# Square roots of the norms moved from ScalarE to four-step Newton iterations on VectorE in a two-layer gated cross-attention kernel

## What is computed

```python
def _layernorm(x, axis=-1, eps=1e-05):
    m = jnp.mean(x, axis=axis, keepdims=True)
    v = jnp.var(x, axis=axis, keepdims=True)
    return (x - m) / jnp.sqrt(v + eps)

x = x + jnp.tanh(g_xattn[0]) * _L0_xattn_ref(_layernorm(x), ctx_1024, ...)
x = x + jnp.tanh(g_ffn[0]) * _L0_ffn_ref(_layernorm(x), ...)
x = x + jnp.tanh(g_xattn[1]) * _L1_xattn_ref(_layernorm(x), ctx_1024, mask, ...)
x = x + jnp.tanh(g_ffn[1]) * _L1_ffn_ref(_layernorm(x), ...)
```

```python
def _ln(t, w, b):
    m = jnp.mean(t, axis=-1, keepdims=True)
    v = jnp.var(t, axis=-1, keepdims=True)
    return (t - m) * jax.lax.rsqrt(v + EPS) * w + b
```

## Time and profile before

| | us |
|---|---|
| time, median of 3 runs | 1687.81 (1685.54 to 1689.53) |
| the profiled execution | 1685.9 |
| its span, first to last instruction | 1684.5 |
| busy in the span: PE, DVE, ACT, POOL | 1454.9, 1229.2, 1127.1, 792.1 |
| mean granted clock of PE | 0.942 of full speed |

### The profile page before, as it was taken

One profiled execution on the slowest core, in us unless ns is written; L12 is line 12 of the kernel. 1 busy time (PEld: TensorE's weight loads), 2 busy tenths in 40 slices (PEclk: granted clock), 3 DMA queues, 4 the chain that ended last, 5 costly groups with the idle time before them and its releaser, 6 DMA issues.

```text
span 1684.5 us, 25330 instructions
## 1 busy us (share of the span) xinstructions
PE 1454.9 (86%) x8374; PEld 711.7 (42%) x8460; DVE 1229.2 (73%) x2184; ACT 1127.1 (67%) x2020; POOL 792.1 (47%) x615
## 2 busy tenths in 40 slices
PE   5687988888888887688898989899899999999979
PEld 3243343343333343244444444344544455455445
DVE  6765766666686356478887768899589997788937
ACT  3567667667764755477787668678477775788724
POOL 3014013014030001078766749787486877577823
PEclk8798997897999999799999999999999999999989
DMA  4001200200340100100000100000000000000000
GB/s 154 1 1 39 43 1 11 50 1 1 60 176 1 51 1 5 39 21 6 1 1 23 38 20 6 26 1 1 6 26 1 26 1 1 1 1 1 1 1 26
DMA packets 20488, 36.69 MB, mean 22 GB/s; under 512 B 4898, under 2 KB 15238, under 8 KB 19334
## 3 DMA queue, kind: packets, MB, share of 16 engines
q1 hardware_dynamic: 20358, 35.07, 7.2%
HBM read 26.53 MB, written 1.15 MB: 16 GB/s over the span
## 4 chain that ended last, share of the span: by engine, by line
PE 35%; POOL 9%; issue 7%; DVE 5%; ACT 3%; POOLq 0%; DMA 0%; ACTq 0%; DVEq 0%; SPq 0%
PE BK L582 35%; POOL arena L1878 6%; DVE arena L1514 3%; DVE arena L1497 1%; ACT arena L1760 1%; ACT arena L1768 1%; POOL arena L1875 1%; POOL arena L1853 1%; ACT arena L1753 1%; POOL arena L1884 1%; POOL arena L1863 1%; DVE arena L886 0%; PE BK L866 0%; ACT L1753 0%; DVE arena L1528 0%
## 5 line engine op out<-in xcount | busy, mean ns | idle before, releaser
L582 PE MATMUL BK<-arena 128*128 128x512 bf16 (+10 forms) x8044 | 1407.2, 378 | 192.6 <-DVE arena L1497 30.6
L582 PEld LDWEIGHTS BK<-arena 128*128 128x128 bf16 (+7 forms) x8130 | 674.2, 115 | 894.8 <-issue 235.1
L1878 POOL TENSOR_TENSOR arena<-arena 128x512 f32<-128x512 f32 (+1 forms) x352 | 509.5, 1447 | 178.6 <-ACT arena L1753 154.5
L1514 DVE TENSOR_TENSOR arena<-arena 128x512 bf16<-128x512 f32 (+1 forms) x416 | 514.4, 1245 | 39.7 <-ACT arena L1760 38.8
L1753 ACT ACTIVATE arena<-BK,arena 128x512 f32<-128x512 f32 (+1 forms) x416 | 285.9, 687 | 132.3 <-PE BK L582 117.1
L1329 DVE TENSOR_REDUCE arena<-BK 128x1 f32<-128x512 f32 x384 | 244.0, 683 | 65.6 <-PE BK L582 64.4
L1661 ACT ACTIVATE arena<-BK 128x512 f32<-128x512 f32 (+1 forms) x416 | 226.0, 598 | 76.0 <-PE BK L582 69.6
L1760 ACT CAST arena<-arena 128x512 bf16<-128x512 f32 (+1 forms) x416 | 253.3, 609 | 0.0
L1768 ACT ACTIVATE arena<-BK 128x512 bf16<-128x512 f32 (+1 forms) x256 | 130.0, 508 | 87.8 <-PE BK L582 86.7
L1497 DVE CUSTOM_DVE_ANT_0 arena<-BK,arena 128x512 bf16<-128x512 f32 (+1 forms) x256 | 145.7, 569 | 47.4 <-PE BK L582 37.5
L1802 POOL TENSOR_TENSOR arena<-arena 128x256 f32<-128x256 f32 (+6 forms) x45 | 30.2, 671 | 208.1 <-ACT arena L1600 205.7
(11 more groups left out here) (170 smaller groups left out, 863.8 us busy)
## 6 DMA issues: line engine op xcount, KB each, us to landing
arena<-arena SPq DMA_DIRECT2D x144, 50.0 KB, 2.2
arena<-in_ctxT SPq DMA_DIRECT2D x8, 800.5 KB, 4.4
arena<-in_ctxk SPq DMA_DIRECT2D x4, 768.0 KB
arena<-in_wo SPq DMA_DIRECT2D x1, 2048.0 KB, 7.9
arena<-in_wqT SPq DMA_DIRECT2D x1, 2048.0 KB, 7.7
arena<-in_x SPq DMA_DIRECT2D x4, 256.0 KB, 11.0
arena<-in_rsel SPq DMA_DIRECT2D x1, 1024.0 KB, 9.2
arena<-in_rw1T SPq DMA_DIRECT2D x1, 1024.0 KB, 5.1
```

The lines of the kernel that those rows point to most:

```text
L582: return T.matmul(out_, lhsT, rhs, start=start, stop=stop, skip_group_check=True)
L1514: V.tensor_tensor(Pl[k][0:m, :], P1[k][0:m, :], Ph[k][0:m, :], ALU.subtract).then_inc(p_low, 1)
L1878: G.tensor_tensor(acc[0:m, g % 2, :], acc[0:m, g % 2, :], P1[k][0:m, :], ALU.add).then_inc(summed1, 1)
```

## The change

- All roots of the head norms but batch 0's are taken on DVE as inverse roots: a first estimate from the bits of the number, and three Newton steps, in four pieces `nw`. The reciprocals of `scale` fall away with them, and POOL's multiplication waits for the root alone.
- Eight of the 16 roots of the x norms (`STEPPED`: turn 1 batches 0 to 2, turn 2 batches 2 and 3, turn 3 batches 0 to 2) are taken the same way in four pieces `nr`.
- The statistics and ACT roots of turn 0 for batches 1 to 3 stand ahead of batch 0's `sqrt`, and x is loaded ahead of the context of batch 1.
- In stage 2 the norms leave `bg` and `og` and have a queue `late` of their own, drawn from in four of every 13 steps. `rest(8)` keeps the places that they had in `bg` empty.

```diff
+STEPPED = ((1, 0), (1, 1), (1, 2), (2, 2), (2, 3), (3, 0), (3, 1), (3, 2))
...
-        to.append(("ln1", turn, b))
-        yield
+        if turn or b == 0:
+            to.append(("ln1", turn, b))
+            yield
+        if (turn, b) in STEPPED:
+            for part in range(4):
+                to.append(("nr", turn, b, part))
+                yield
...
-            for _ in range(2 if b else 1):
-                yield
-            piece("sqrt", b)
             if b:
                 yield
+                yield
+                for part in range(4):
+                    piece("nw", b, part)
+                    yield
+            else:
+                for later in range(1, B):
+                    piece("ln1", 0, later)
+                yield
+                piece("sqrt", b)
...
-        bg = chain(context(1), values(1), masked(1), self.norm(to, 2, 2), self.norm(to, 2, 3), context(2), values(2),
+        bg = chain(context(1), values(1), masked(1), rest(8), context(2), values(2),
...
-        og, paced = iter(()), [0]
+        og, late, paced = iter(()), chain(self.norm(to, 2, 2), self.norm(to, 2, 3)), [0]
...
-                og = chain(finish(g - 1), self.norm(to, 3, (g - 1) // 8) if g % 8 == 0 else None)
+                og = finish(g - 1)
+                if g % 8 == 0:
+                    late = chain(late, self.norm(to, 3, (g - 1) // 8))
...
+            if kt % 13 in (11, 12, 0, 1):
+                next(late, None)
...
+        def dve_root_step(x, y, t, part, done):
+            dve.wait_ge(dve_chain.sem, dve_chain.n)
+            if part == 0:
+                V.tensor_scalar(y.bitcast(I32), x.bitcast(I32), -0.5, 1597463007.0, ALU.mult,
+                                ALU.add).then_inc(dve_chain.sem, dve_chain.up())
+            else:
+                V.tensor_tensor(t, y, y, ALU.mult).then_inc(dve_chain.sem, dve_chain.up())
+                dve.wait_ge(dve_chain.sem, dve_chain.n)
+                V.scalar_tensor_tensor(out=t, in0=t, scalar=-0.5, in1=x, op0=ALU.mult,
+                                       op1=ALU.mult).then_inc(dve_chain.sem, dve_chain.up())
+                dve.wait_ge(dve_chain.sem, dve_chain.n)
+                u = V.scalar_tensor_tensor(out=y, in0=t, scalar=1.5, in1=y, op0=ALU.add, op1=ALU.mult)
+                u.then_inc(*((done, 1) if part == 3 else (dve_chain.sem, dve_chain.up())))
+
+        def dve_norm_root(turn, b, part):
+            sl = slice(2 * b, 2 * b + 2)
+            if part == 0:
+                dve.wait_ge(stat1, 8 * (turn - 1) + 2 * b + 2)
+                V.tensor_scalar(rsq[:, sl], mv[:, sl, 1], 1e-5, None, ALU.add).then_inc(dve_chain.sem, dve_chain.up())
+            dve_root_step(rsq[:, sl], rst[:, sl], rtt[:, :], part, root1)
...
+                elif kind == "nw":
+                    b, part = arg
+                    x, t = (sq[:, k, :].rearrange("p (k h) -> p k h", h=H) for k in range(2))
+                    if part == 0:
+                        for j in range(5):
+                            dve.wait_ge(*summed(5 * b + j))
+                        V.tensor_scalar(x, ss[:, :, :], 1.0 / 16, 1e-6, ALU.mult,
+                                        ALU.add).then_inc(dve_chain.sem, dve_chain.up())
+                    dve_root_step(x, ss[:, :, :], t, part, ss_root)
...
-            SP.dma_start(ctxT[:, 1, :], a["ctxT"][1]).then_inc(ld_ctx[1], 16)
             for b in range(1, B):
                 SP.dma_start(x_sb[:, 2 * b:2 * b + 2, :], xv[:, 2 * b:2 * b + 2, :]).then_inc(ld_x[b], 16)
+            SP.dma_start(ctxT[:, 1, :], a["ctxT"][1]).then_inc(ld_ctx[1], 16)
```

More of the change, by code:

```diff
@@ L8 @@
 U8 = mybir.dt.uint8
+I32 = mybir.dt.int32
 ALU = mybir.AluOpType
@@ L429, in finish, with rest @@
                     yield
+        def rest(n):
+            for _ in range(n):
+                yield
         for _ in values(0):
             pass
-        bg = chain(context(1), values(1), masked(1), self.norm(to, 2, 2), self.norm(to, 2, 3), context(2), values(2),
+        bg = chain(context(1), values(1), masked(1), rest(8), context(2), values(2),
                    context(3), values(3), masked(2), ternary(0), masked(3), ternary(1, 2))
-        og, paced = iter(()), [0]
+        og, late, paced = iter(()), chain(self.norm(to, 2, 2), self.norm(to, 2, 3)), [0]
         mgs = chain(*[gen(g + n) for g in range(NG) for gen, n in ((self.maxima, 1), (self.qproj, 2)) if g + n < NG])
@@ L467, in stage2 @@
             pace(2)
-        for _ in chain(og, finish(NG - 1), bg):
+        for _ in chain(og, late, finish(NG - 1), bg):
             pass
@@ L595, in program @@
         rsq = sb("rsq", [128, NT])
+        rtt = sb("rtt", [128, 2])
         xn = sb("xn", [128, 2, D])
@@ L835, in dve_norm_apply @@
             dve.wait_ge(root1, 4 * (turn - 1) + b + 1) if turn else dve.wait_ge(root0, b + 1)
-            V.reciprocal(rst[:, sl], rsq[:, sl]).then_inc(dve_chain.sem, dve_chain.up())
-            dve.wait_ge(dve_chain.sem, dve_chain.n)
+            if (turn, b) not in STEPPED:
+                V.reciprocal(rst[:, sl], rsq[:, sl]).then_inc(dve_chain.sem, dve_chain.up())
+                dve.wait_ge(dve_chain.sem, dve_chain.n)
             if turn and norm_before(turn, b):
@@ L1253, in vector_main @@
                     dve_norm_stats(*arg)
+                elif kind == "nr":
+                    dve_norm_root(*arg)
                 elif kind == "ln2":
                     dve_norm_apply(*arg)
+                elif kind == "nw":
[7 more added lines that the diff above has]
+                    dve_root_step(x, ss[:, :, :], t, part, ss_root)
                 elif kind == "kv":
@@ L1285, in vector_main @@
                     lo, hi, m = ((14, 16, 128), (0, 4, 128), (4, 8, 128), (8, 12, 128), (12, 14, TAIL))[r]
-                    dve.wait_ge(ss_root, b + 1)
-                    V.reciprocal(ss[:, lo:hi, :], ss[:, lo:hi, :]).then_inc(ss_recip, 1)
                     if b == 0:
+                        dve.wait_ge(ss_root, 1)
+                        V.reciprocal(ss[:, lo:hi, :], ss[:, lo:hi, :]).then_inc(ss_recip, 1)
                         v = kc[0:m, lo:hi, :].rearrange("p k (h d) -> p (k h) d", d=16)
@@ L1577, in scalar_main @@
                 i, n = slot.get(piece, (None, None))
-                if kind == "ln1":
+                if kind == "ln1" and arg not in STEPPED:
                     act_norm_root(*arg)
@@ L1599, in scalar_main @@
                     act.wait_ge(*summed(u - 2)) if u >= 2 else act.wait_ge(rsb_done, 1)
+                    act.wait_ge(ss_root, b)
                     A.activation(sq[0:m, 4 * k:4 * k + hi - lo, :], kc[0:m, lo:hi, :], ACT.Square).then_inc(squared, 1)
@@ L1811, in gpsimd_main @@
                     v = kc[0:m, lo:hi, :].rearrange("p k (h d) -> p (k h) d", d=16)
-                    pool.wait_ge(ss_recip, 5 * b + r + 1)
+                    pool.wait_ge(ss_root, b + 1)
                     G.tensor_tensor(v, v, ss[0:m, lo:hi, :].rearrange("p k h -> p (k h)").unsqueeze(2)
```

## The result

The median of four runs is 1716.26 us (1708.12 to 1717.68), beside 1688.67 for the kernel before: a ratio of 1.016, 95% interval 1.0139 to 1.0181. The change costs 27.6 us, where a gain of 10.3 was forecast, and the time lies outside the range. The profiled execution (1708.1, span 1706.7) is the fastest of the four. Its mean granted clock is 0.937; the other three have 0.928 or 0.929, and the profiled execution of before (1685.9) had 0.942.

What follows compares the result with a forecast made beforehand. PE was taken to set the end in both attentions. The terms -10.3 - 6 + 3.7 + 4 - 3.2 + 1.5 gave -10.3 us, from 1685.9 to 1675.6, or 1677.5 us as median; range 1660 to 1692.

Steps and rivals of the forecast that it cites:

- Start: Before batch 0's root: statistics of batches 1 to 3 and a narrow root delay it, +3.7 us, ends 3.2 and 4.0.
- the sign was 45.6: Start of the kernel: the head root of batch 0 would begin near 45.6 us, not 41.9.
- ACT visits of stage 0: Nine ACT roots with table loads between exponentials, where PE stands, go from stage 0: -10.3 us, good end -15.5.
- the 9 loads: ACT table loads: 9 remain of 37, none between 100 and 577 us but for the last norm.
- no shorter than 479 us although the visits are gone: Stage 0: the prediction would be wrong if it lasted at least 479 us with the ACT root visits gone.
- DVE in stage 0: Root work moved to DVE in stage 0, net 12.4 us, mostly hidden: +4 us, ends 0 and +12.4.
- DVE in stage 2: Five narrow roots add 10 us to DVE in stage 2, mostly hidden: +1.5 us, ends 0 and +10.
- Clock: PE's half-clock stretches behind visits in stage 0 partly come back: -6 us, ends 0 and -20.4.
- Late queue: Stage 2: the new queue spreads each norm over two groups; the move was priced at nothing.
- Stage 2 visits: Five ACT roots with table loads go from stage 2, less PE's usual idle share: -3.2 us.
- DVE takes ACT's place: Rival: all 22.4 us of added DVE links lie on the path, clock gives nothing: +12.6, 1700 us; chance 0.17.

Runs made afterwards that it cites:

- c3: Kernel before with only the turn 0 statistics and roots moved ahead of batch 0, every root on ACT: 1683.81 us, ratio 0.9979.
- d2: d1 with one Newton step in place of three in each wide head root, so head norms are not exact: 1670.02 us, ratio 0.9878.
- d1: c1 with the three wide head roots by Newton on DVE, with as many yields as before: 1685.35 us, ratio 0.9977.
- d3: c1 with the five narrow roots of stage 2 by Newton on DVE: 1698.44 us, ratio 1.0051.
- c1: Changed kernel without any Newton step, all roots on ACT; only the late queue and the early start kept: 1676.61 us, ratio 0.9918.
- d4: d3 with eleven one-input reciprocals in place of each narrow Newton root, the five roots left out: 1675.46 us, ratio 0.9935.
- a1: Changed kernel with the norms of turns 2 and 3 as before, roots on ACT and in `bg` and `og`: 1704.34 us, ratio 1.0102.
- a2: Changed kernel with the roots of turns 2 and 3 on ACT, late queue kept: 1692.72 us, ratio 1.004.
- c2: Kernel before with the late queue of stage 2 alone, every root on ACT: 1680.64 us, ratio 0.9955.
- a3: Changed kernel with the four `nw` pieces at two places, so preparation has as many yields as before: 1713.0 us, ratio 1.0153.
- b1: Changed kernel with all eight narrow Newton roots replaced by chains of eleven reciprocals, the roots left out: 1694.66 us, ratio 1.0031.
- c4: c1 with the three narrow roots of turn 1 by Newton on DVE: 1678.2 us, ratio 0.9937.
- c5: c4 with the turn 0 statistics and roots back in each batch's preparation: 1678.0 us, ratio 0.9939.

## Why the prediction was wrong

- **Start, +3.7: right.** The first exponential is 3.3 us later. The head root of batch 0 began at 44.56 us, where the sign was 45.6. As a whole the start is still a gain of 0.2% (c3). The sum's own terms, +3.7 and a third of the -10.3, had it about even.
- **ACT visits of stage 0, -10.3: the waits fell as forecast**, 24.6 to 13.5, where I had said some 13, and the 9 loads are right. It was given back through DVE and the late rows: stage 0 took 483.7 us, and "no shorter than 479 us although the visits are gone" was the prediction's own sign of being wrong.
- **DVE in stage 0, +4: mis-sized.** The DVE time itself was right: 317.5 us in stage 0 where 305.1 stood, 12.4 more. I took a third of it. PE's waits for maxima rose by 19.4 us, not by 4. Alone the wide roots lose 8.7 net of their visits' gain, and d2 against d1 says that 18 wide instructions of 0.42 us, 7.6 us of DVE, cost 15.3 us: not a third of DVE's time counts, but nearly twice all of it. That DVE was idle for 36% of the stage said nothing, for the wide parts stand just ahead of the maxima.
- **DVE in stage 2, +1.5, bounds 0 and +10: the step that failed most.** Its price of 0.20 us came from a row of the wrong kind, a reciprocal with one input, though two-input instructions were what the diff adds. What failed is that row as the price, and that most of it would be hidden: the 55 instructions take 24.7 us of DVE and not 10, and the move costs +22 (d3 against c1) where visits and DVE together had -1.7. With one-input instructions in their places the cost is gone (d4 against d3, 20 to 23 us). DVE's busy time in stage 2 grew by only 9.7 us, near the 10 priced: the busy share did not show it. The trace of before could have warned me. Its line 1514 (1569 after), with two SBUF inputs, lasts 0.69 us in one step and nearly twice that in the next, with a mean of 1279 ns over 382:

```profile
766.17 0.69 DVE L1514 TENSOR_TENSOR arena<-arena 128x512 bf16<-128x512 f32 x1 [0.41 <-ACT arena L1760]
...
767.76 1.30 DVE L1514 TENSOR_TENSOR arena<-arena 128x512 bf16<-128x512 f32 x1 [0.51 <-ACT arena L1760]
```

  One shape with two durations was the sign that something other than its width sets them.
- **Clock, -6: wrong sign.** The share at half clock grew over the whole, mean clock 0.942 to 0.937 and, in the other three runs, 0.928 or 0.929. In the profiled execution stage 0 has 79 us at half clock in place of 92, but a1 and a2, with the same stage 0, have 106 and 113; stage 2 has 68 in place of 46. The stretch of 395 to 412 us that I looked at is at full clock now, but others came, one of 17 us around PE's wait for the late row at 461 us.
- **Late queue, 0: a gain of 7.6 us by itself** (c2). I did not look for it, and its cause stays open.
- **SP not priced.** `kd` and the rows share a queue; the sum had no term for what is moved on it. PE's wait for the row grew by 11.2 us; what it costs in the end, 3.3 us by medians (a3), is not clear of noise.
- **Stage 2 visits, -3.2: not settled.** d4 has none of the five and c1 has all, and they can't be told apart (1675.5 and 1676.6), but d4 has 55 links instead. PE idles for 66 us of stage 2 in both. The idle share behind this term was also read too high, since the earlier trace rows lack 75 of 4184 matmul records.
- **The rival "DVE takes ACT's place"**, 1700 us with a chance of 0.17, had the side right. Its mechanism was that every link counts. For stage 2 that is not the main cost: with the same 55 links, of one SBUF input each, the loss over c1 is gone (d4), and all 88 narrow ones are 21.6 us cheaper than Newton's (b1). For the wide roots of stage 0 it held: there DVE's time is what costs (d1 against d2).

The rule of "VectorE: DVE Perf Modes" of the Trainium skill (Rules for kernel authors) on few chained instructions would have given the right side, too. The runs show that in stage 2 the count is not the main cost: d4 has as many as d3 and is 23 us faster. Rows 13 also hold one width only, so they could not say that a step costs 0.2 us whatever its width; the wide ones took 0.42 and 0.29 us.

## What to carry to other kernels

Before work goes to DVE, list its instructions by their inputs and look at what POOL does in the same steps: in these traces one with two SBUF inputs was priced not by its width, but by the POOL instruction that it stood behind, and everything queued behind it on DVE waited as well. Price a stall of PE at its idle time and the half-clock stretch that follows. And test the parts of a change alone: here the two that had been priced at nothing or about even, the queue and the start, are the gain (1676.6 us), and the part that was its purpose is the loss.

## What was not expected of the hardware

- A 128x2 instruction on DVE that took up to 1.62 us, ended each time with a POOL instruction, while a reciprocal of the same shape stayed at 0.15 to 0.17 us beside the same POOL work.
- Runs of one kernel differ with the mean clock: before had 1681.5 us at 0.949 and 1692.6 at 0.933 in one comparison. Parts worth 5 us are hard to see in that: c1, c4, c5 and d4 can't be told apart. Even one stage of one program differs, 483.7 to 493.5 us for stage 0 of the change, by its time at half clock.
